# Attention scores of layers 1 and 3: from two 64-row matmuls per head pair to full 128-row matmuls against zero-padded queries

## The reference, cut to what matters

```python
# layer 1
q = xn @ Wq;  kv = cn @ Wkv;  k, v = jnp.split(kv, 2, axis=-1)
q, k, v = (reshaped to b, heads 8, rows 256, 64)
sim = jnp.einsum('bhid,bhjd->bhij', q, k) * scale
attn = jax.nn.softmax(sim, axis=-1)
out = jnp.einsum('bhij,bhjd->bhid', attn, v)
# layer 3
k_x = rope_rotate_k(k_x)          # k * cos + neg_half(k) * sin
k = jnp.concatenate([k_x, k_l], axis=2)
v = jnp.concatenate([v_x, v_l], axis=2)
sim = jnp.einsum('bhid,bhjd->bhij', q, k)   # q already times scale
```

## Time and profile before

| | us |
|---|---|
| median of 3 runs | 1868.16 |
| their range | 1861.4 to 1869.75 |
| the profiled execution | 1862.23 |
| its span, first to last instruction | 1860.5 |
| TensorE matmul busy | 1693.1 (91%) |
| VectorE busy | 1091.3 (59%) |
| ScalarE busy | 681.6 (37%) |
| GpSimd busy | 258.4 (14%) |

### The profile page before, as it was taken

One profiled execution on the slowest core, in us unless ns is written; L12 is line 12 of the kernel. 1 busy time (PEld: TensorE's weight loads), 2 busy tenths in 40 slices (PEclk: granted clock), 3 DMA queues, 4 the chain that ended last, 5 costly groups with the idle time before them and its releaser, 6 DMA issues. The chain is left out here.

```text
span 1860.5 us, 28250 instructions
## 1 busy us (share of the span) xinstructions
PE 1693.1 (91%) x9431; PEld 1236.4 (66%) x9431; DVE 1091.3 (59%) x3250; ACT 681.6 (37%) x1747; POOL 258.4 (14%) x277
## 2 busy tenths in 40 slices
PE   6889778799998999999887799999889999999799
PEld 4667546567766568888676578887656665656575
DVE  5988866568787532232368571002356777676666
ACT  5877842454454211111133222221133443344331
POOL 2100131211022100000232120000120001010115
PEclk9999989999999999999899899999989999999999
DMA  8854042211012325454353875335221111011363
GB/s 250 254 184 134 7 128 68 80 37 36 28 58 81 110 90 170 153 165 169 102 170 117 292 285 176 114 124 176 57 86 43 43 44 50 26 35 29 103 190 113
DMA packets 170926, 212.91 MB, mean 114 GB/s; under 512 B 17081, under 2 KB 137506, under 8 KB 170658
## 3 DMA queue, kind: packets, MB, share of 16 engines
q1 hardware_dynamic: 159730, 183.57, 30.7%
q0 software_dynamic: 10496, 27.28, 4.6%
q10 hardware_dynamic: 560, 0.27, 0.1%
HBM read 148.95 MB, written 57.92 MB: 111 GB/s over the span
## 5 line engine op out<-in xcount | busy, mean ns | idle before, releaser
L788 POOL DMA_INDIRECT slots_in<-f_xn,f_slot x88 | 85.0, 966 | 465.1 <-DVE f_slot L562 441.3
L3506 PE MATMUL r_bank<-r_w,r_hT 128*128 x624 | 139.3, 379 | 1.0 <-DVE r_hT L3650 1.0
L3506 PEld LDWEIGHTS r_bank<-r_w,r_hT 128*128 128x128 f32 x624 | 118.4, 190 | 22.8 <-issue 7.5
L1498 ACT ACTIVATE a_probs<-a_s,a_negmax 128x512 f32<-128x512 f32 x128 | 86.9, 684 | 103.7 <-DVE a_negmax L1746 103.7
L1347 PEld LDWEIGHTS a_t<-kept_ident,a_probs 128*128 128x128 f32 x768 | 83.1, 142 | 61.8 <-issue 38.8
L1331 PE MATMUL a_s<-a_kT,a_qT 64*128 64x256 f32 (+1 forms) x512 | 109.1, 524 | 14.2 <-ACT a_probs L1504 7.6
L3591 DVE TENSOR_TENSOR r_y<-r_bank,r_b_row 128x256 f32<-128x256 f32 (+1 forms) x27 | 14.7, 543 | 177.5 <-PE r_bank L3506 177.2
L3121 PE MATMUL r_bank<-r_xgT,r_firsts 128*128 128x256 f32 x512 | 113.2, 379 | 0.0
L2283 DVE CUSTOM_DVE_ANT_0 a_s<-a_s,a_mask_bias 128x256 f32<-128x256 f32 x256 | 100.5, 454 | 20.3 <-PE a_s L2110 20.1
L1746 DVE TENSOR_REDUCE a_negmax<-a_s 128x1 f32<-128x512 f32 x128 | 82.2, 683 | 49.7 <-PE a_s L1331 49.1
L1347 PE MATMUL a_t<-kept_ident,a_probs 128*128 128x128 f32 x768 | 106.4, 281 | 2.0 <-DVE a_probsT L1764 1.6
(11 more groups left out here) (424 smaller groups left out, 3408.3 us busy)
## 6 DMA issues: line engine op xcount, KB each, us to landing
r_firsts<-in_f_w SPq DMA_DIRECT2D x27, 1024.0 KB, 5.1
r_firsts<-in_f_w SPq DMA_DIRECT2D x46, 512.0 KB, 4.3
slots_in<-a_zeros SPq DMA_DIRECT2D x8, 2048.0 KB, 12.6
half_in<-a_zeros SPq DMA_DIRECT2D x8, 1024.0 KB, 9.7
r_w<-in_f_w SPq DMA_DIRECT2D x8, 1024.0 KB, 7.0
a_share_of<-shares_out SPq DMA_DIRECT2D x28, 256.0 KB, 3.9
r_xg<-slots_in SPq DMA_DIRECT2D x28, 256.0 KB, 2.9
slots_out<-r_y SPq DMA_DIRECT2D x28, 256.0 KB, 2.1
```

What stands on the lines that cost most here:

```text
L788: pool.indirect_dma_start(self.slots_in[:, :], bass.IndirectOffsetOnAxis(ap=self.slot[:, c, tile:tile + 1], axis=0), src, None).then_inc(s ...
L1498: last = nc.scalar.activation(probs[:, g % PROBS, i, :], bank[:, :], ACT.Exp, bias=negmax[:, g % 4, i, 0:1], accum_out=sum_of(e, h, t_only))
L3506: last = nc.tensor.matmul(d_bank[:, t * D:(t + 1) * D], hT[:, j % 2, m, t * P:(t + 1) * P], slots.second[:, bass.ds(e, 1), m, :], start=(m ...
```

## The change

- `qT` gets a plane for each head of a block (`[P, 2, GROUPS, NC_, SEQ]`, twice its size). Plane g holds the queries of head g on their 64 partitions, and zeros on the other 64. GpSimd clears these zeros once per layer, with two memsets of 64 partitions by 2048 elements, behind its first gathers; it then waits for both.
- ScalarE writes the queries with two instructions of 64 partitions for each bank, where one of 128 did it. The first waits for the memsets.
- `scores` multiplies all 128 rows of `kT` with plane i of `qT`; the zeros cancel the other head. The number of matmuls, their columns and banks stay. The loop over heads is now outside that over query tiles.
- In layer 3, the product with cos is written into `kT`, and `k_turn` is added to it there; `k_cos` is gone.

```diff
-        qT = sb("qT", [P, 2, PACK, NC_, SEQ])
+        assert PACK == 1 and GROUPS == 2
+        qT = sb("qT", [P, 2, GROUPS, NC_, SEQ])
...
-            k_cos = sb("k_cos", [P, 2, 2, SEQ])
...
-                    nc.gpsimd.tensor_tensor(kT[:, 0, 2 * j:2 * j + 2, 0:SEQ], k_cos[:, j, :, :], k_turn[:, j, :, :],
+                    nc.gpsimd.tensor_tensor(kT[:, 0, 2 * j:2 * j + 2, 0:SEQ], kT[:, 0, 2 * j:2 * j + 2, 0:SEQ], k_turn[:, j, :, :],
                                             ALU.add).then_inc(rope_done, 1)
...
             if head is not None:
                 for e in range(GATHERS_AHEAD):
                     head.pool_gather(pool, e)
+            for g in range(GROUPS):
+                others = slice((1 - g) * R, (2 - g) * R)
+                pool.memset(qT[others, :, g, :, :], 0.0).then_inc(q_cleared, 1)
+            pool.wait_ge(q_cleared, GROUPS)
             if cfg.rope:
                 rotate_first()
...
-                for t in (t_only,) if WIDE else range(TB):
-                    for i in range(2):
-                        g = 2 * pair + i
-                        rows = slice(g * R, (g + 1) * R)
-                        c, m = blk // PACK, blk % PACK
+                for i in range(2):
+                    for t in (t_only,) if WIDE else range(TB):
                         out = banks[i][:, :] if WIDE else banks[i][:, t * SEQ:(t + 1) * SEQ]
-                        last = nc.tensor.matmul(out, qT[rows, e % 2, m, c, t * P:(t + 1) * P], kT[rows, e % 2, c, :],
+                        last = nc.tensor.matmul(out, qT[:, e % 2, i, blk, t * P:(t + 1) * P], kT[:, e % 2, blk, :],
                                                 start=True, stop=True)
...
-                    last = nc.scalar.activation(qT[:, e % 2, 0, 2 * j:2 * j + 2, :],
-                                                bank[:, :].rearrange("p (c n) -> p c n", c=2), ACT.Copy, scale=cfg.scale)
+                    if e == 0 and j == 0:
+                        act.wait_ge(q_cleared, GROUPS)
+                    for g in range(GROUPS):
+                        own = slice(g * R, (g + 1) * R)
+                        last = nc.scalar.activation(qT[own, e % 2, g, 2 * j:2 * j + 2, :],
+                                                    bank[own, :].rearrange("p (c n) -> p c n", c=2), ACT.Copy, scale=cfg.scale)
...
-                    nc.vector.tensor_tensor(kT[:, e % 2, 2 * j:2 * j + 2, 0:SEQ], k_cos[:, j, :, :], k_turn[:, j, :, :],
-                                            ALU.add).then_inc(rope_done, 1)
+                    keys = kT[:, e % 2, 2 * j:2 * j + 2, 0:SEQ]
+                    nc.vector.tensor_tensor(keys, keys, k_turn[:, j, :, :], ALU.add).then_inc(rope_done, 1)
...
-                    for dst, turn in ((k_cos, cos), (k_sin, sin)):
-                        last = nc.vector.tensor_tensor(dst[:, j, :, :], chunks, turn[:, :].unsqueeze(1).to_broadcast([P, 2, SEQ]),
+                    for dst, turn in ((kT[:, e % 2, 2 * j:2 * j + 2, 0:SEQ], cos), (k_sin[:, j, :, :], sin)):
+                        last = nc.vector.tensor_tensor(dst, chunks, turn[:, :].unsqueeze(1).to_broadcast([P, 2, SEQ]),
                                                        ALU.mult)
```

More of the change, by code:

```diff
@@ L1056, in tiled_attention @@
         max_ready = sem("max_ready")
+        q_cleared = sem("q_cleared")
         o_full = sem("o_full")
```

## The result

The changed kernel takes **1907.95 us**, median of 4 runs (1903.13 to 1911.59). The kernel before takes 1867.38 us (4 runs, 1861.40 to 1869.75). The ratio is 1.0221, with a 95% interval of 1.0184 to 1.0257: slower by 40.6 us. The forecast was 1916, with a range of 1893 to 1937. The profiled execution after took 1903.13 us with a span of 1901.4, so the two profiled executions differ by 40.9 us, and that is what the traces can divide.

What follows compares the result with a forecast made beforehand. TensorE was taken as the bound in both attention layers: 40.6 (layer 3) + 21.7 (layer 1) - 15.3 (idle time) + 0.5 (queries) = 47.5 us, on 1862.2 gives 1909.7, plus 5.9 for the median: 1916 us, range 1893 to 1937.

Steps and rivals of the forecast that it cites:

- The bound and the scores' price: Attention of layers 1 and 3: TensorE sets the pace; each step's scores grow from 1.06 to 1.76 us, +0.70.
- The 2x: Scores matmuls: the skill page's speedup of up to 2x would make them 2.12 us, the whole change about 79 us.
- rival B: 64-row form also costs neighbours 0.2 us a step; layer 3's opening at full clock, up to 3 us; 1894; chance 0.10.
- The idle time: TensorE's waits in both attention layers each shrink by up to 0.70 us; in all 15.3 us come back.
- The memsets: GpSimd in both layers' openings: 3.6 us for both memsets, ending before the queries need them; cost 0.
- My bound for a memset twice as dear: Layer 1's opening: were a memset twice as dear, the layer would pay about 1.3 us.
- Queries, keys, loop order: Split queries add 19 us of ScalarE, only +0.5 us in layer 1's opening; in-place keys cost 0; loop order saves nothing.
- The six covered steps: Last six steps of layer 3: TensorE waits for late VectorE, so their longer scores cost nothing; 58 of 64 pay.
- the forecast's own bounds: Whole kernel's growth: 89 x 0.66 - 20 = 39 us to 96 x 0.76 - 9 = 64 us.
- A: Both attention layers: waits only move along, all 96 steps pay 0.76 us, cost 73 us, 1941 us; chance 0.07.
- C: Chain through VectorE sets the step; longer matmuls hidden, 0.18 us off each of 96 steps, 1851 us; chance 0.03.
- D: Scores: the zeros or the form cost nothing; time within 0.5% of 1868 us; chance 0.03.

## Why the prediction was right, and where its terms were not

**The bound and the scores' price: right.** The steps lengthened where TensorE was the bound. Eight steps of layer 3, as many as a batch has, took 49.11 us before (1491.63 to 1540.74) and 52.45 after (1518.29 to 1570.74). Their eight groups of scores took 8.48 and 14.23 us: +0.72 a step, where I took 0.70. In layer 1 four steps (454.88 to 483.74 before, 468.61 to 499.86 after) have four groups, 4.26 and 7.32 us: +0.77, at the upper end of my 0.76. The reason given (two heads on different rows share the time) was an argument in the prediction; the kernel with both heads on the same rows shows it. That kernel's 1.91 us also stand 0.2 us above the 1.72 of a group that leaves no form, which is the size of the remainder that I had worked out for entering and leaving it. The 2x stayed out of the sum rightly: 1.06 us became 1.72 to 1.83, 1.6 to 1.7 times.

**What the neighbours give back: missed.** This was half of rival B, priced at nothing in the sum. In the same eight steps of layer 3, the transposes take 7.78 and 7.07 us and the projections 17.92 and 17.50: together 1.13 us in eight steps, 0.14 a step. In the four steps of layer 1 the transposes take 3.72 and 3.49, and the projection of line 1301 takes 3.67 and 3.44, 0.11 a step. I had priced the old group at its own start and end, and so left in its neighbours what the change of form costs them. The two middles (below) show it whole. In layer 3's 48 steps the scores grew by 34.35 us (50.88 to 85.23), the idle time fell by 7.93 (11.45 to 3.52), and the stretch grew by 18.87, so the neighbours gave back 34.35 - 7.93 - 18.87 = 7.55 us, 0.16 a step. In layer 1's 24 steps it is 18.32 - 3.37 - 12.45 = 2.50 us, 0.10 a step. Together 10 us. The transposes kept their 0.93 us in the kernel with the rows put back and in the one with both heads on the same rows, so it is the 64*128 form that their longer time goes with.

**The idle time: right in kind, a little too much.** I let 19 waits of layer 3 give 9.2 of 11.4 us. The idle time went to 3.5 us, so it gave 7.9, and below 4 us is what I asked of the profile; in the eight steps above, waits of 1.25 us became 0.00. In layer 1's middle it gave 3.4 where I had put 4.7. Capping each wait at one step's growth came out as a fair rule, some 1.3 us too generous in each.

**The clock in layer 3's opening: named in rival B, not in the sum.** Timeline of TensorE before, then after, and busy time of one stretch of after:

```profile
1381.64 0.63 PE L1347 MATMUL a_t<-kept_ident,a_probs 128*128 128x128 f32 x4 [1.61 <-DVE a_probsT L1764]
...
1386.89 1.97 PE L1347 MATMUL a_t<-kept_ident,a_probs 128*128 128x128 f32 x8
1388.65 4.92 PE L1271 MATMUL a_s<-a_xT,kept_weights 128*128 128x256 f32 x16
```

```profile
1408.74 1.04 PE L1349 MATMUL a_t<-kept_ident,a_probs 128*128 128x128 f32 x8
1409.61 3.62 PE L1276 MATMUL a_s<-a_xT,kept_weights 128*128 128x256 f32 x16
```

```profile
1404.00:1412.00 8.00, 6.05 (x32) 4.32 (x30) 7.43 (x16) 4.37 (x11) 0.00 (x0) 1.00 0.69 224
```

Before, two waits of 0.42 and 1.61 us stand ahead of 1382, and the clock from 1382 to 1390 is 0.65. After, the longer scores have filled both waits, and in the counterpart, from 1404 to 1412 us, the clock is 1.00 with as much idle time as before (2.0 us). The transposes and the projection are 0.9 and 1.3 us shorter there (1.76 to 0.87, and 4.85 to 3.55 us, start to start), and even the scores ahead of them are, 2.01 us at the lower clock (1384.88 to 1386.89) and 1.79 after. The other kernels agree. In the same stretch, 12 to 20 us behind layer 3's first scores, the clock is between 0.57 and 0.79 in all eight profiles with the short scores, and 1.00 in all three with the long ones: the changed kernel, the one whose zeros VectorE writes, and the one with both heads on the same rows. From the first scores to the fifth group's successor, 1370.04 to 1393.50 before and 1391.96 to 1413.16 after, the changed kernel is 2.3 us *faster*, with four of its five groups longer. I had counted five steps there at 0.70, less 1.4 us for the two waits behind 1382, and those two stayed (1.11 and 0.84 us); the two ahead of it went, which I had not looked at.

**The memsets: wrong.** The step said "Cost 0" because nobody waits for the memsets and GpSimd's queue had room. Both hold. It asked who waits for GpSimd, and not who works in SBUF beside it: VectorE was held up for 2.5 us, and TensorE's clock was low behind the gap, together 4.1 of the 4.9 us by which the opening grew. My bound for a memset twice as dear, 1.3 us, used the same wrong rule. The size itself was right, 1.85 us each in the trace. In layer 3, a memset meets VectorE's line 262 in the same way, but there it moves GpSimd's adds off line 217:

```profile
1373.69 0.16 DVE L217 SCALAR_TENSOR_TENSOR a_rstd<-a_moments,a_rstd 128x2 f32<-128x2 f32 x1
1373.89 2.33 DVE L262 TENSOR_SCALAR a_xn<-kept_x,a_moments,a_rstd 128x256 f32<-128x256 f32 x2
```

One is 1.6 us longer, the other 1.8 us shorter, and the opening stays, -0.2. The zero that I forecast there came out, for a reason that I did not give.

**Queries, keys, loop order: right.** One half of a query instruction costs 591 ns, the full price that I took. The opening pays 0.6 us for it, against 0.5. The in-place add takes 687 ns, as the one into another tile did. In the kernel before, exchanging the loops changes nothing.

**The sum, piece by piece.** The forecast's column is its own terms set in the place where they belong: 0.70 for each step that pays, less what the waits there were to give back.

| piece | forecast | measured |
|---|---|---|
| layer 1, opening | +0.5 | +4.9 |
| its first 4 steps | +2.8 | +1.8 |
| its 24 steps of the middle | 16.8 - 4.7 = +12.1 | +12.5 |
| its last 4, and the end | +2.1 | +1.8 |
| layer 3, opening | 0 | -0.2 |
| its first 5 steps | 3.5 - 1.4 = +2.1 | -2.3 |
| its 48 steps of the middle | 33.6 - 9.2 = +24.4 | +18.9 |
| its last 11, and the end | +3.5 | +1.2 |
| everything else | 0 | +2.2 |
| sum | +47.5 | +40.8 |

Layer 3's middle is 5.5 us short: 7.6 us from the neighbours the one way, and scores that grew by 34.4 and not 33.6 (0.8) with idle time that gave 1.3 less the other. Its first steps are 4.4 us short, the clock and the two filled waits. Layer 1's opening is 4.4 us over, the memsets. In layer 1's middle, scores that grew by 1.5 more than I took, neighbours that gave back 2.5, and idle time that gave 1.3 less nearly cancel.

The end of layer 3 is 2.3 us cheaper than I took it. I had counted six steps as covered by TensorE's waits. First the busy time of the output projection behind the longest of them, in the kernel before; then the timeline of the same projection after:

```profile
1728.30:1733.54 5.24, 5.24 (x16) 4.23 (x17) 2.05 (x4) 1.45 (x4) 0.00 (x0) 0.67 0.01 3
...
1769.53 3.72 PE L1403 MATMUL a_t<-kept_weights,a_o_raw 128*128 128x256 f32 x16 [1.93 <-DVE a_o_raw L1692]
```

The wait of 4.02 us became 1.93, and one of 2.85 us for `f_xT`, which ended at 1748.36 in the kernel before, became 1.53, ending at 1788.06. The projection took 5.24 us at a clock of 0.67 and takes 3.56 at 1.00 (1769.53 to 1773.09). So eleven steps at 0.72 are 7.9 us, less 3.4 from these waits, 1.7 from the clock and some 1.5 from the neighbours (11 x 0.14): an estimate of 1.3, where 1.2 was measured. That is as far as it can be told: the two profiles of the kernel before differ by 1.3 us behind their last scores. The six covered steps, 4.2 us in the forecast, gave 3.4; the clock and the neighbours were the terms missing, as in the first steps.

So the terms that I had too high in layer 3 and the one that I had too low in layer 1 have opposite signs, and that the number came out so near is in part luck. The growth of 40.6 us is just above the 39 us that was the lower end of the forecast's own bounds, before the part of rival B; without the 4.4 us of the memsets it would have been 36, outside them. The single time, 8 us high as it is, would then have been 12 us high.

Of the rivals, A (nothing comes back), C (the chain is the bound) and D (no effect) are out: the waits shrank, the time grew by what TensorE grew, and the form alone carries it. B was right in kind: 0.10 to 0.16 a step and not 0.20, and the clock.

## What to carry to other kernels

Zeros in place of unused rows of a contraction are not free on TensorE where the two halves can run side by side: pairs of 64-row matmuls on different rows took 1.06 us for what 128 rows with zeros take 1.72 to 1.83. Price a change of form with its neighbours too, by a whole batch from start to start, and look at the granted clock behind each wait that the change makes shorter or longer. And when work is added to an idle GpSimd, look at what VectorE does in that stretch, whether or not a semaphore links them; here the same zeros cost 4 us less from VectorE itself, in a gap.

## What the runs showed of the hardware beside this

- A memset of 64 partitions costs GpSimd as much as one of 128: 1.85 us each for 2048 float32 elements, against 1.8 us in the earlier trace rows. VectorE took 1.76 us for the same.
- Of VectorE's work beside a GpSimd memset, only the 128x256 `TENSOR_SCALAR` were held up (0.81 to 2.38, and 0.74 to 1.71 us a pair). In layer 3's opening two copies of 128x512 out of a bank took 1.27 us together beside a memset, and 1.28 in the kernel before. Beside a GpSimd add of two tiles, a 128x2 operation with two inputs took 1.93 us and not 0.16.
- Two matmuls on different rows shared the time even when those of one head were written next to each other (1.07 us for the group in either order): the second head's matmuls then start 0.01 us behind the first head's, ahead of matmuls written before them.
- A gap of TensorE cost more than its length here: 2.5 us more of waiting were followed by a stretch at 0.57 of the full clock that cost another 1.6 us. And longer matmuls that filled waits of 0.42 and 1.61 us kept the clock at 1.00 where it had been 0.65.
